# Four elementwise additions per pair of tiles move from GpSimd to VectorE in a clamped low-rank linear kernel

## The reference: what is computed

```python
W = weights[condition]                       # condition: 128 indices in 0..15, one per batch item
y = jnp.einsum('bct,bcd->bdt', x, W)         # x: (128, 64, 1024)
z = jnp.einsum('bsd,od->bso', y, Wf) + b     # Wf: 1024 x 1024
u = jnp.einsum('bsd,edr->ebsr', y, A)        # 8 x 16 = 128 low-rank columns
m = jnp.einsum('ebsr,ero,e->bso', u, B, p_scores)
gamma = jnp.minimum(0.5 * norm(z) / (norm(m) + 1e-6), 1.0)   # norms over the last axis
out = x + z + gamma * m
```

## Time and profile before

| | |
|---|---|
| median of 3 runs | 945.18 us (944.28 to 945.48) |
| the profiled execution | 945.04 us, of which the span of its instructions is 943.2 us |
| TensorE matmul busy | 917.3 us (97%) |
| VectorE busy | 571.8 us (61%), 889 instructions |
| ScalarE busy | 355.5 us (38%) |
| GpSimd busy | 338.9 us (36%), 326 instructions |
| mean granted TensorE clock | 0.991 of full |
| one pair in the steady part | 28.26 us |

### The profile page before, as it was taken

The page is one execution under the profiler, slowest core; times in us unless marked ns, Lnnn a source line. Parts: engine busy times, 40 slices in busy tenths (PEclk is TensorE's granted clock), DMA queues, the critical chain, the costliest instruction groups (busy, mean ns, idle before and its releaser), DMA issues. The chain is left out here.

```text
span 943.2 us, 15151 instructions
## 1 busy us (share of the span) xinstructions
PE 917.3 (97%) x4888; PEld 790.1 (84%) x4888; DVE 571.8 (61%) x889; ACT 355.5 (38%) x694; POOL 338.9 (36%) x326
## 2 busy tenths in 40 slices
PE   7979999999999999999999999999999999999995
PEld 5768888888888888888888888888888888888884
DVE  3976555656555656555656555656555656555653
ACT  4443433433432433432433432433432433432431
POOL 1353323443323443323443323443323443323442
PEclk9989999999999999999999999999999999999998
DMA  9022112222112222112222112222112222112201
GB/s 328 13 71 92 45 72 92 92 69 91 45 69 92 92 69 91 46 69 92 92 69 91 46 69 92 92 69 91 46 69 92 92 69 91 46 69 92 93 23 67
DMA packets 32455, 75.16 MB, mean 80 GB/s; under 512 B 12729, under 2 KB 13754, under 8 KB 32442
## 3 DMA queue, kind: packets, MB, share of 16 engines
q1 hardware_dynamic: 32120, 74.93, 22.3%
q10 hardware_dynamic: 322, 0.07, 0.0%
HBM read 41.42 MB, written 33.55 MB: 79 GB/s over the span
## 5 line engine op out<-in xcount | busy, mean ns | idle before, releaser
L410 ACT CAST y_hi<-mix_ps 128x512 fp32r<-128x512 f32 x128 | 75.5, 591 | 320.9 <-PE mix_ps L776 320.9
L340 POOL TENSOR_TENSOR stats<-stats 128x1 f32<-128x1 f32 x32 | 17.7, 554 | 455.6 <-ACT squares L457 455.6
L617 DVE TENSOR_TENSOR s_lo<-s,s_hi 128x512 fp32r<-128x512 f32 x124 | 134.3, 1103 | 4.2
L776 PEld LDWEIGHTS mix_ps<-mixer,x_in 128*128 128x128 f32 x1024 | 125.6, 193 | 12.4 <-issue 6.9
L776 PE MATMUL mix_ps<-mixer,x_in 128*128 128x128 f32 x1024 | 126.7, 277 | 6.0 <-DMA mixer<-in_L_cond_weights_dram 3.4
L326 POOL TENSOR_TENSOR z<-z,x_in 128x512 f32<-128x512 f32 x64 | 82.8, 1294 | 118.6 <-ACT squares L438 118.6
L596 DVE TENSOR_TENSOR y_lo<-mix_ps,y_hi 128x512 fp32r<-128x512 f32 x128 | 87.9, 687 | 55.4 <-ACT s L416 41.2
L423 ACT CAST s_hi<-s 128x512 fp32r<-128x512 f32 x124 | 76.6, 618 | 114.2 <-POOL s L314 97.9
L789 PE MATMUL b_ps<-w_hi,y_hi 128*128 128x512 f32 x256 | 101.1, 395 | 6.4 <-DVE z L682 6.4
L789 PE MATMUL b_ps<-w_lo,y_hi 128*128 128x512 f32 x256 | 100.7, 393 | 0.0
L789 PE MATMUL b_ps<-w_hi,y_lo 128*128 128x512 f32 x256 | 100.3, 392 | 0.0
(11 more groups left out here) (110 smaller groups left out, 1846.1 us busy)
## 6 DMA issues: line engine op xcount, KB each, us to landing
x_in<-in_x_dram SPq DMA_DIRECT2D x64, 512.0 KB, 3.7
out_dram<-z SPq DMA_DIRECT2D x64, 512.0 KB, 2.7
w_hi_raw<-in_L_ffn_W_dram SPq DMA_DIRECT2D x8, 256.0 KB, 6.8
w_lo_raw<-in_L_ffn_W_dram SPq DMA_DIRECT2D x8, 256.0 KB, 7.3
mixer<-in_L_cond_weights_dram SPq DMA_DIRECT2D x124, 16.0 KB, 2.1
a_lo_raw<-in_L_ffn_A_dram SPq DMA_DIRECT2D x1, 512.0 KB, 8.5
bias<-in_L_ffn_b_dram SPq DMA_DIRECT2D x1, 512.0 KB, 8.2
b_lo_raw<-in_L_ffn_B_dram SPq DMA_DIRECT2D x1, 512.0 KB, 8.1
```

The costliest lines, as they stand in the source:

```text
L340: nc.gpsimd.tensor_tensor(stat(NORM_Z, 1), stat(Z_SQ, 1), half, ALU.pow).then_inc(norm_z_ready[1], 1)
L410: nc.scalar.copy(y_part(y_hi, r, h), mixed(h)).then_inc(y_hi_ready, 1)
L617: nc.vector.tensor_tensor(s_lo[:, n, :, :], s_raw(n), s_hi[:, n, :, :].bitcast(fp32), ALU.subtract).then_inc(s_lo_ready, 1)
L776: made = nc.tensor.matmul(mix_ps[:, h, k * P:(k + 1) * P], x_in[:, slot, (h * HC + k) * P:(h * HC + k + 1) * P], mixer[:, r, :], start=Tru ...
```

## The change

VectorE takes over all of GpSimd's wide instructions. GpSimd keeps the norms. `make_s1` and `make_s4` stand on VectorE right behind `make_s2`. `residual1(p - 1)` stands behind the split of S2, ahead of `make_gamma(p - 1, 1)`. `residual0(p - 1)` becomes one instruction of 128x1024 and stands behind the addition to `z1[:, lo]` that waits for p4, ahead of `make_gamma(p - 1, 0)`. It increments `residual0_ready` by 2, and SP, TensorE and ScalarE are as before.

```diff
 @block.gpsimd, step
                     if not opening:
                         norm_z1(p - 1)
-                        residual1(p - 1, 2 * (1 - j) + 1)
                         norm_m(p - 1, 1)
-                        make_s1(p)
                         norm_z0(p - 1)
-                        residual0(p - 1, 1 - j, 1)
-                        make_s4(p)
-                    residual0(p, j, 0)
-                    if not opening:
                         norm_m(p - 1, 0)
...
 @block.vector
+            def make_s1(p):
+                dve.wait_ge(s2_made, p)
+                nc.vector.tensor_tensor(s14[:, 0, :, :], s23[:, 0, :, :], s14[:, 0, :, :], ALU.add).then_inc(s1_made, 1)
...
+            def residual1(p, slot):
+                dve.wait_ge(z1_squared, p + 1)
+                nc.vector.tensor_tensor(z1[:, :], z1[:, :], x_in[:, slot, :], ALU.add).then_inc(residual1_ready, 1)
+
+            def residual0(p, par):
+                dve.wait_ge(z11_squared, p + 1)
+                dve.wait_ge(z12_squared, p + 1)
+                nc.vector.tensor_tensor(z0[:, par, :], z0[:, par, :], x_in[:, 2 * par, :],
+                                        ALU.add).then_inc(residual0_ready, 2)
...
 @block.vector, step
                     split_s(p, S2)
+                    residual1(p - 1, 2 * (1 - j) + 1)
                     make_gamma(p - 1, 1)
                     add_m1(p - 1)
...
                     nc.vector.tensor_tensor(z1[:, lo], a_ps[:, :], bias[:, 2, :], ALU.add).then_inc(p4_biased, 1)
+                    residual0(p - 1, 1 - j)
                     make_gamma(p - 1, 0)
                     add_m0(p - 1, 1 - j, m_ps[:, :])
...
                         make_s2(p + 1, False)
+                        make_s1(p + 1)
+                        make_s4(p + 1)
...
             steps(dve, step)
+            residual1(PAIRS - 1, 3)
             make_gamma(PAIRS - 1, 1)
             add_m1(PAIRS - 1)
             make_z12(PAIRS - 1, 1)
+            residual0(PAIRS - 1, 1)
             make_gamma(PAIRS - 1, 0)
```

More of the change, by code:

```diff
@@ L305, in _ @@
         def _(pool):
[L306 to L327, removed]
             def norm_z0(p):
@@ L373, in _ @@
             norm_m(PAIRS - 1, 1)
-            residual1(PAIRS - 1, 3)
             norm_m(PAIRS - 1, 0)
             norm_z0(PAIRS - 1)
-            residual0(PAIRS - 1, 1, 1)
         @block.scalar
@@ L612, in make_s2, with make_s4 @@
                 nc.vector.tensor_tensor(s23[:, 0, :, :], mixed(1), s23[:, 1, :, :], ALU.subtract).then_inc(s2_made, 1)
+            def make_s1(p):
+                dve.wait_ge(s2_made, p)
+                nc.vector.tensor_tensor(s14[:, 0, :, :], s23[:, 0, :, :], s14[:, 0, :, :], ALU.add).then_inc(s1_made, 1)
+            def make_s4(p):
+                nc.vector.tensor_tensor(s14[:, 1, :, :], s14[:, 1, :, :], s23[:, 0, :, :],
+                                        ALU.subtract).then_inc(s4_made, 1)
+            def residual1(p, slot):
[6 more added lines that the diff above has]
+                                        ALU.add).then_inc(residual0_ready, 2)
             def split_s(p, n):
@@ L720, in _ @@
             make_s2(1, True)
+            make_s1(1)
+            make_s4(1)
             split_t(T1)
```

## The result

The changed kernel takes 1117.87 us in the median of 4 runs (1114.87 to 1119.83), the kernel before beside it 945.33 us. The ratio is 1.1814 with a 95% interval of 1.1797 to 1.1832; the medians lie 172.5 us apart. The forecast was 1099 us, with a range of 1064 to 1138.

What follows compares the result with a forecast made beforehand. TensorE's own matmuls were taken to bound the kernel at 28.26 us a pair. From 945.04 us: stalls +126, clock +30, head +0.1, tail -2.0, giving 1099 us, range 1064 to 1138.

Steps and rivals of the forecast that it cites:

- What bounds the kernel: Steady pairs: TensorE's matmuls fill all 28.26 us, so savings on other engines can gain only in head and tail.
- S1 and S4 at no cost: VectorE ahead of p3: two additions of 0.68 us fill 1.27 us of idle time, costing TensorE nothing.
- `residual1` at no cost: VectorE ahead of p2: a 1.2 us addition leaves 0.3 to 0.4 us of 1.6 us slack, costing nothing.
- The splits: VectorE's splits of S3, S1, S4: at 0.6 us each without GpSimd beside them, ending about 460.3 instead of 461.1.
- `residual0`: Behind VectorE's wait for p4: delays SP's x load 9.9 us, stalling TensorE's tile 0 mix 4.2 us, 30 times, 126 us.
- the chain that I put at 4.6 us: Tile 0, from SP's issue of the x load to the landing of its second mixer part: 4.6 us, ends 4.4 and 5.2.
- the two chains of the earlier trace: x issue to mixer landing: 4.7 us for tile 1, 5.2 for tile 0; the forecast went by tile 1.
- The clock: Behind each stall of TensorE: granted clock falls in part, 1.0 us per stall as mean, 30 us (0 to 63).
- The price of one fall: A TensorE product on the low clock takes 4.87 us instead of 2.75, so a fall costs up to 2.1 us.
- Rival 1: The clock falls in every stall and costs its full price: 1132 us, 1150 with the long chain; chance 0.20.
- Head and tail: First pair +0.1 us; tail -2.0 us (-1.7 to -2.8), from the waits for GpSimd's last residuals.
- Rivals 2 to 4: Clock holds, 1069 us (chance 0.23); load hidden, 943.1 us (0.03); VectorE late ahead of p2, 949 to 956 us (0.02).

Runs made afterwards that it cites:

- e1: Changed kernel with `residual0(p - 1)` moved up, behind the split of S4 and ahead of the addition that waits for p2: 942.74 us, ratio 0.9965.
- e3: Changed kernel with `residual0` back on GpSimd in two halves; S1, S4 and `residual1` stay on VectorE: 944.74 us, ratio 0.999.
- e6: Changed kernel with 12 extra unused matmuls of 128x256 ahead of TensorE's `mix_next_0` in each pair: 1117.21 us.
- e7: Changed kernel with SP's index reads and mixer loads of tile 0 ahead of its wait for `residual0` and the x load: 1060.68 us.

## Why the prediction was right, and where it was off

What bounds the kernel: right. Nothing changed the 28.26 us of a pair as long as TensorE didn't wait (e1, e3), whichever engine had the work.

S1 and S4 at no cost: right. They fill VectorE's idle time ahead of p3 to the tenth. `residual1` at no cost: right; the slack left ahead of p2 is 0.47 us, and its 128x1024 addition takes 1.22 us, as I took from rows 7. The splits, now without GpSimd beside them, take 1.89 us for three in place of 3.84, and since nobody waited for them that is worth nothing.

`residual0`: the step on which all rests, right in place and in size. Taken from the issue of x to the mix, the chain that I put at 4.6 us took 519.91 - 515.45 = 4.46 us. Forecast 4.2 us per stall (4.0 to 4.8), 126 us; the rows of the changed kernel give 4.03 for the one followed above, and the kernels with a filled stall 4.2 and 125 us over before. The choice between the two chains of the earlier trace rows was right too: from x to the first mixer load tile 0 now takes 1.19 us, about as tile 1 did, against 1.79 before.

The clock: right in kind, too small in size. It makes 17.5 of the 19 us by which the forecast is low: I took 30 us, 1.0 per stall as a mean over falls and none, from a price of up to 2.1; the runs give 47.5 us in all, 1.6 per pair, because the clock fell behind 29 of the 30 stalls. Their frequency was the term that I had mis-sized. The argument for it, that a stall of 4.1 us is about as long as the clock took to fall in the head (3.6 and 3.9 us), was a poor guide: in the changed kernel the fall came mostly 4.7 to 5.3 us behind the last matmul, when TensorE was at work again, and e6 shows it in nearly each pair with an idle time of 2.5 us. The total lies in the range because the range was wide enough for a fall at nearly each stall, not because the mean of 1.0 us was well founded.

The price of one fall, up to 2.1 us, was read from the product at 61.17 in the earlier trace rows (it is p2, and not p1 as the prediction says). In the kernel before, the lower clock lasts there up to 65.4:

```profile
58.70:65.40 6.70, 4.22 (x10) 3.36 (x11) 4.06 (x7) 0.62 (x1) 2.26 (x2) 0.50 0.46 160
```

So TensorE worked at half the clock for over 4.2 us there, and for about 3.3 us (520.8 to 524.1) behind the stall followed above; half of the latter, an estimate of 1.65 us, agrees with the 1.6 measured. Rival 1 (each stall drops the clock) was right on the frequency and too high on the price, 1132 us. By the rule of the Trainium skill ("TensorE: Matmul & The Clock Gate", the table under "Why this matters for your kernels") that was cited for that rival each stall would lower the clock; the trace agrees for 29 of 30 stalls in the changed kernel. In e7, with an idle time between those of e6 and of the changed kernel, the clock falls behind 13 of 30.

Head and tail: forecast +0.1 and -2.0 us. e1, which has no stall, is 2.6 us faster than before (its profiled span 2.3: 940.9 against 943.2), but the parts fell otherwise. Of the 2.3 us, 1.1 are gone ahead of the tail: VectorE's addition behind p7 of the last pair stands at 925.24, where it stood at 926.30. They come from the first pair. First the wait of PE ahead of the mix of the second pair in e1, then VectorE's two additions for T1 there:

```profile
44.06 2.26 PE L775 MATMUL mix_ps<-mixer,x_in 128*128 128x128 f32 x16 [1.10 <-DVE y_lo L565]
```

```profile
30.83 2.35 DVE L529 TENSOR_TENSOR w_lo_raw<-w_lo_raw,w_hi_raw 128x1024 f32<-128x1024 f32 x2
```

That wait was 2.19 us before, and 2.19 in e3, where GpSimd still makes the first half of `residual0` of pair 0 at that time (from 32.41 to 33.85 in e3). I had taken 2.36 us for two such additions from the earlier trace rows and not looked at the two that stand beside GpSimd's, which took 3.44 us before, and 3.44 in e3. So in the head, where TensorE does wait for VectorE, it gains by GpSimd's silence what it gains nowhere in the steady part. The tail of e1 behind the last product:

```profile
930.90 0.15 DVE L620 TENSOR_SCALAR stats<-stats 128x1 f32<-128x1 f32 x1 [0.95 <-POOL stats L322]
...
931.61 1.28 DVE L640 SCALAR_TENSOR_TENSOR z<-m_ps,stats,z 128x1024 f32<-128x1024 f32 x1
...
936.57 1.28 DVE L633 SCALAR_TENSOR_TENSOR z<-mix_ps,stats,z 128x1024 f32<-128x1024 f32 x1
```

From the addition behind p7 to the last one it is 11.33 us (936.57 - 925.24), against 12.61 before (938.91 - 926.30, the second in the earlier trace rows): 1.3 us gained in place of 2.0. The residuals no longer hold the additions of gamma x m up, but GpSimd's root does.

Rivals 2 to 4 have no support: no pair but the last kept its clock, the load was not hidden, and TensorE doesn't wait ahead of p2.

What stays open: what decides whether an idle time of 2.5 to 3 us lowers the clock. Its length alone doesn't: about 2.5 us did it 29 times in 30 in e6, and 2.4 to 3.1 us 13 times in 30 in e7. The pairs of e6 and of the changed kernel have the same mean length, 34.1 us, those of e7 don't; a kernel that holds the idle time fixed and changes the pair's length alone would test it, and wasn't run.

## What to carry to other kernels

When an instruction moves to another engine, ask first what is released by its end, and which waits stand ahead of its new place: here an addition of 1.2 us, moved behind a wait for a product of the same pair, pulled a prefetch of 4.5 us out from under TensorE. The right place on the same engine costs nothing, and the whole change with this one line moved (e1) beats the kernel before by 2.6 us. And a stall that repeats in TensorE can have a second price in the clock behind it, here more than a third of the first. How often it is paid can't be read from the length of the stall alone: 29 times in 30 at 3.9 and at 2.5 us, 13 times at 2.9 and never at 1.0.

## What I had not expected of the hardware

Idle times of 2.5 us of TensorE in each pair of 34 us went with the lower clock in 29 of 30 pairs, while 1.0 us brought none; useless matmuls that shortened the idle time from 3.9 to 1.0 us made the kernel 47.6 us faster. SP's first mixer load came 1.79 us behind the x load where a 512 KB store had been issued just ahead of both the earlier trace rows, and 1.19 us behind it in the changed kernel, where none had; that the store is the cause wasn't tested by itself.

Two 128x1024 additions of VectorE took 3.44 us beside GpSimd's addition in the first pair before, and less than 2.4 without it; three 128x512 splits took 3.84 us beside GpSimd's wide additions and 1.89 without them.
